# Second pass of the attention scores as two half-height products

## What is computed

```python
q, k, v = (_split_heads(query @ W) for W in (Wq, Wk, Wv))
w = jnp.einsum('bhqd,bhkd->bhqk', q, k) / DH
w = w + causal[None, None]
w = jax.nn.softmax(w, axis=-1)
mask = jnp.clip((tmpl + span_val * attn_span) / (RAMP + 1), 0.0, 1.0)
w = w * mask
w = w / (jnp.sum(w, axis=-1, keepdims=True) + 1e-08)
out = jnp.einsum('bhqk,bhkd->bhqd', w, v)
return out.transpose(0, 2, 1, 3).reshape(out.shape[0], s, H * DH) @ Wo
```

## Time and profile before

| | |
|---|---|
| median of 3 runs | 3855.66 us (3855.27 to 3858.33) |
| the profiled execution | 3857.66 us |
| its span, first to last instruction | 3855.9 us |
| PE busy (matmul) | 3504.2 us, 91% |
| PEld busy (weight loads) | 3151.9 us, 82% |
| DVE busy | 3002.8 us, 78% |
| ACT busy | 2365.9 us, 61% |
| POOL busy | 820.8 us, 21% |
| mean granted TensorE clock | 0.980 |

### The profile page before, as it was taken

How to read it: one execution, slowest core, us unless ns; L and a number is a source line. 1 busy time by engine, 2 the same in 40 slices (tenths; PEclk the granted TensorE clock), 3 DMA queues, 4 the chain that set the end, 5 groups by cost and what they waited for, 6 DMA issues and landing times. The chain is left out here.

```text
span 3855.9 us, 90130 instructions
## 1 busy us (share of the span) xinstructions
PE 3504.2 (91%) x29924; PEld 3151.9 (82%) x29924; DVE 3002.8 (78%) x4884; ACT 2365.9 (61%) x5622; POOL 820.8 (21%) x830
## 2 busy tenths in 40 slices
PE   0899996999999899989989998998999999599998
PEld 0899995888788788878878887887888888499998
DVE  7899984777777777777777777777777777599996
ACT  1454543676677667667767766776776777344544
POOL 2223221111122112112211211221121121123232
PEclk8999998999999999999999999999999999799999
DMA  6111114444534444444434444444444444211110
GB/s 211 63 55 52 54 36 129 102 102 105 130 96 118 103 116 111 108 119 99 121 97 116 114 110 114 98 119 100 116 114 102 110 109 109 92 40 51 57 49 34
DMA packets 162617, 374.13 MB, mean 97 GB/s; under 512 B 19696, under 2 KB 61552, under 8 KB 161776
## 3 DMA queue, kind: packets, MB, share of 16 engines
q1 hardware_dynamic: 162288, 370.30, 37.1%
HBM read 129.31 MB, written 39.58 MB: 44 GB/s over the span
## 5 line engine op out<-in xcount | busy, mean ns | idle before, releaser
L1233 ACT ACTIVATE at_eT_hi<-at_t_ps 128x512 f16<-128x512 f32 (+3 forms) x1536 | 745.3, 492 | 564.4 <-PE at_t_ps L1145 520.2
L1314 DVE SCALAR_TENSOR_TENSOR at_eT_lo<-at_t_ps,at_eT_hi 128x512 f16<-128x512 f32 (+3 forms) x1536 | 826.1, 551 | 163.0 <-ACT at_eT_hi L1233 132.6
L1225 ACT ACTIVATE at_e_rows<-at_s_ps,at_neg_max 128x1024 f32<-128x1024 f32 (+7 forms) x1024 | 767.0, 749 | 127.2 <-DVE at_neg_max L1308 126.3
L1145 PE MATMUL at_t_ps<-at_ident,at_e_rows 128*128 128x128 f32 x4608 | 778.8, 278 | 52.0 <-DVE at_eT_lo L1314 46.6
L1308 DVE TENSOR_REDUCE at_neg_max<-at_s_ps 128x1 f32<-128x1024 f32 (+7 forms) x1024 | 766.6, 749 | 41.8 <-PE at_s_ps L1135 30.4
L1131 PE MATMUL at_s_ps<-at_kh_st,at_q_st 128*128 128x512 f32 (+2 forms) x1536 | 581.1, 378 | 52.3 <-issue 25.4
L1159 PE MATMUL at_o_ps<-at_v_cols,at_eT_hi 128*128 128x130 f16 x4608 | 608.1, 221 | 19.0 <-ACT at_o_raw L1241 17.5
L1145 PEld LDWEIGHTS at_t_ps<-at_ident,at_e_rows 128*128 128x128 f32 x4608 | 503.6, 141 | 90.8 <-DVE at_eT_lo L1314 67.3
L1159 PE MATMUL at_o_ps<-at_v_cols,at_eT_lo 128*128 128x65 f16 x4608 | 566.8, 192 | 0.0
L1132 PE MATMUL at_s_ps<-at_kl_st,at_q_st 128*128 128x512 f32 (+2 forms) x1536 | 515.1, 343 | 0.0
L1159 PEld LDWEIGHTS at_o_ps<-at_v_cols,at_eT_hi 128*128 128x128 f16 x4608 | 434.0, 98 | 35.7 <-ACT at_o_raw L1241 21.7
(11 more groups left out here) (184 smaller groups left out, 7336.7 us busy)
## 6 DMA issues: line engine op xcount, KB each, us to landing
at_kh_st<-at_k_hi SPq DMA_DIRECT2D x256, 256.0 KB, 4.4
at_kl_st<-at_k_lo SPq DMA_DIRECT2D x256, 256.0 KB, 5.9
at_w_qk<-w_qk_split SPq DMA_DIRECT2D x65, 512.0 KB, 6.2
at_q_st<-at_q_hi SPq DMA_DIRECT2D x128, 256.0 KB, 3.9
at_q_st<-at_q_lo SPq DMA_DIRECT2D x128, 256.0 KB, 4.9
at_w_v<-w_v_split SPq DMA_DIRECT2D x66, 256.0 KB, 5.7
at_w_out<-w_out_split SPq DMA_DIRECT2D x64, 256.0 KB, 5.7
ffn_x_rows<-in_L_attn_query_dram SPq DMA_DIRECT2D x32, 256.0 KB, 2.8
```

The lines of the kernel that those rows point to most:

```text
L1145: last = nc.tensor.transpose(t_ps[i % 2][:, b * P:(b + 1) * P], e_rows[:, n % 4, (k0 + b) * P:(k0 + b + 1) * P], ident[:])
L1225: nc.scalar.activation(e_rows[:, n % 4, :w], s_ps[n % 2][:, col:col + w], ACT.Exp, bias=neg_max[:, n % 4:n % 4 + 1], accum_out=e_sum[:, pa ...
L1233: nc.scalar.activation(eT[0][:, i % EBUF, :count * P], t_ps[i % 2][:, :count * P], ACT.Copy, scale=PSCALE).then_inc(sem("eT_hi"), 1)
L1314: nc.vector.scalar_tensor_tensor(out=eT[1][:, i % EBUF, :count * P], in0=t_ps[i % 2][:, :count * P], scalar=PSCALE, in1=eT[0][:, i % EBUF, ...
```

## The change

The second pass of units with two chunks is written anew; units with one chunk keep theirs. A new set of tiles, `q_low`, gets a copy of q_hi in rows 64 to 127. In a two-chunk unit all first-pass products come first, then the mask product, then two products of 64 rows each: chunk 0 with q_hi and k_lo from rows 0 to 63 (`q_st`, `kl_st`), chunk 1 with q_hi and k_lo from rows 64 to 127 (`q_low`, `kl_st`). They write different banks of `s_ps`. The term q_lo k_lo is no longer added in these units. `place` issues two more copies for each pair, between those of q_lo and the wait for k_lo, and PE's counts for `q_placed` rise from 4 to 6 copies.

```diff
@@ -865,6 +865,7 @@
         q_st, kh_st, kl_st = ([[sb(f"{n}{i}{a}", [P, SEQ], F32R) for a in range(2)] for i in range(2)] for n in ("q_st", "kh_st", "kl_st"))
+        q_low = [[sb(f"q_low{i}{a}", [P, SEQ], F32R) for a in range(2)] for i in range(2)]
@@ -915,7 +916,7 @@
             def place(g, par):
 
-                for n, tiles in (("q", [(q_st, 0, 0), (q_st, 1, 1)]), ("k", [(kh_st, 0, 0), (kh_st, 0, 1), (kl_st, 1, 0), (kl_st, 1, 1)])):
+                for n, tiles in (("q", [(q_st, 0, 0), (q_st, 1, 1), (q_low, 0, 1)]), ("k", [(kh_st, 0, 0), (kh_st, 0, 1), (kl_st, 1, 0), (kl_st, 1, 1)])):
                     sp.wait_ge(sem(f"{n}_lo"), 2 * g + 2)
@@ -1119,20 +1120,26 @@
-                    pe.wait_ge(sem(f"q_placed{par}"), g * 32 + (64 if par == 0 else 32))
+                    pe.wait_ge(sem(f"q_placed{par}"), g * 48 + (96 if par == 0 else 48))
                     pe.wait_ge(sem(f"k_placed{par}"), g * 64 + (128 if par == 0 else 64))
 
                 pe.wait_ge(sem("exp_done"), g * NU + (n - 1 + AHEAD["exp_done"]))
                 chunks = score_chunks(j)
+                tile = slice(j * P, (j + 1) * P)
                 for ci, (col, k0, w) in enumerate(chunks):
-                    lastc = ci == len(chunks) - 1
                     out = s_ps[n % 2][:, col:col + w]
-                    qs = q_st[par][a][:, j * P:(j + 1) * P]
+                    qs = q_st[par][a][:, tile]
                     nc.tensor.matmul(out, qs, kh_st[par][a][:, k0:k0 + w], start=True, stop=False)
-                    last = nc.tensor.matmul(out, qs, kl_st[par][a][:, k0:k0 + w], start=False, stop=not lastc)
-                    if lastc:
+                    if len(chunks) == 1:
+                        nc.tensor.matmul(out, qs, kl_st[par][a][:, k0:k0 + w], start=False, stop=False)
+                    if ci == len(chunks) - 1:
                         diag = col + j * P - k0
-                        last = nc.tensor.matmul(s_ps[n % 2][:, diag:diag + P], ident_b[:], causal[:], start=False, stop=True)
+                        last = nc.tensor.matmul(s_ps[n % 2][:, diag:diag + P], ident_b[:], causal[:], start=False, stop=len(chunks) == 1)
+                if len(chunks) == 2:
+                    for ci, (col, k0, w) in enumerate(chunks):
+                        rows = slice(ci * DH, (ci + 1) * DH)
+                        last = nc.tensor.matmul(s_ps[n % 2][:, col:col + w], (q_st, q_low)[ci][par][a][rows, tile], kl_st[par][a][rows, k0:k0 + w],
+                                                start=False, stop=True)
                 last.then_inc(sem("scores_done"), 1)
```

## The result

The changed kernel takes 3939.99 us (median of 4 runs, 3939.1 to 3942.85), the kernel before beside it 3856.43: 83.6 us or 2.2% slower, ratio 1.0217, 95% interval 1.02 to 1.0235. The forecast was 3931, in a range from 3790 to 4000. The profiled execution has a span of 3937.3 us.

The account below looks back on a forecast made before the run. PE's own stream was taken as the bound. Per head 0.01 + 0.24 + 8 x 0.05 = 0.65 us, times 128 = 83, less a tenth for waits +75, plus 1 for copies: 3855.66 becomes about 3931, range 3790 to 4000.

Parts of the forecast that it names:

- column saving of 0.65 us for a head: Second passes of a head's four long tiles: fully side by side, 1.52 us becomes 0.87, saving 83 us over 128 heads.
- max(first, 0.11 + second): Pair of half products in a two-chunk unit: loads in line, so pairs take 0.23, 0.23, 0.29, 0.34 us.
- Late loads: At changes of tile no load is pulled ahead: 0.11 us shows going in, 0.06 at the transpose going out.
- the row at the mask product: Trace of the kernel before: the mask's 2-byte load begins with its product (1517.18 both), after 0.28 us of idle load path.
- the 0.32 us of the earlier trace: Kernel before, loads at 1502.77 and 1502.88: a held product starts 0.32 us from the next instead of 0.23.
- d: Time the array needs to run empty at each change of tile: taken as 0.05 us, eight changes a head.
- a tenth: PE's waits for DVE and ACT shrink when PE comes later, absorbing this share: 83 us becomes +75.
- Copies: Two more q copies per pair, some 0.6 us each, hidden with 3 us to spare; +1 us once at the start.
- (a): Rival: loads and tile changes free enough; 3821 with loads in line (chance 0.24), 3785 with loads side by side (0.13).
- (c): Rival: halves pass one after another, only changes add; 3876 with everything pulled ahead, 3986 with late loads; chance 0.06.
- (d): Rival: heavy tile changes, emptying at its upper bound of 0.16 us each; +196 us, 4050; chance 0.05.
- (b): Rival: even, changes cheap but loads late, or overlap just pays for the changes; 3848 to 3863; chance 0.09.

Follow-up runs that it names:

- the run with the mask product first: Kernel before, no half products or copies; mask product moved to the head of units following short products or transposes: 3851.0 us, ratio 0.9986.
- the run with the order alone: Changed kernel with its order and copies, but the second pass on all 128 rows: 3883.03 us, ratio 1.0072.
- mask last: Changed kernel with the mask product behind the half products instead of ahead of them: 3917.82 us, ratio 1.0162.
- pairs twice: Changed kernel with each pair of half products issued twice within one stay at half height: 4053.16 us, ratio 1.0509.

## Why the prediction was right

**The bound.** PE's stream was the bound and a change of it counted nearly in full, at an unchanged clock: right.

**Overlap.** The column saving of 0.65 us for a head was right: putting both halves on the same rows gave back 85.7 us, where 83 were computed. But the step that let the second half load follow 0.11 behind the first (a pair's time of max(first, 0.11 + second), 1.09 us a head) failed. Loads of different halves start together, and the pairs take their wider width, 0.87.

**Late loads.** No load is pulled ahead across a change of tile: right, and the row at the mask product led to it, though as an analogy it holds only behind score products (see the last section). Its size held too, 0.10 to 0.11 for a 4-byte load and 0.06 for a transpose. One reading was wrong: the 0.32 us of the earlier trace rows is not a late load. That unit follows transposes, the last of which was still passing; behind value products, where 0.32 stands as well (1509.93 to 1510.25), the load is late. The sum does not rest on it, the run with the mask product first did. The 0.05 that falls to the order of the mask product and not to the change of tile was inside the sum but in the wrong place; the run with the order alone (+23.5 us) showed it.

**Running empty.** d was put at 0.05, between 0 and 0.16. Measured 0.09 going in (mask last, the kernel in which nothing else stands there) and 0.10 going out (pairs twice). This term was mis-sized, 8 x 0.05 for a head instead of 8 x 0.095, so 46 us too small over 128 heads. Against it stood the in-line loads, 0.22 x 128 = 28 us too much, and the half load going in, put down at 0.11 where 0.10 was measured, 5 us too much. The rule of the Trainium skill, TensorEngine Tiling (Array Packing), Key Properties, that a change of mode drains TensorE, agrees with these 0.09 and 0.10 us; it gives no price.

**The sum.** Visits as measured cost 4 x 0.35 = 1.40 us a head, less 0.65 is 0.75, times 128 is 96 us; of the measured 83.6 us the copies are about 4, so 79 of the 96 arrived, and waits took a sixth of it, where a tenth was put down. Where they did can be added up from the two traces: from the first score product to the end of the transposes the units with two chunks take 92 us more, and the start of these units comes 12 us later behind the work ahead of it; the units with one chunk, which the change leaves alone, take about 18 us less, because their transposes start sooner behind the mask product (22 us less in all). The forecast's visits of 1.30 us a head, less 0.65, gave 83. That 3931 and 3940 lie so near is thus partly luck: two terms erred in opposite directions.

**Copies.** Hidden in the steady stretch, as said: right. The queue's wait for k in the changed kernel is still there:

```profile
SPq L923 <- DVE at_k_lo L1283: 190.4, 63, 3.3
```

3 us for each pair remain. At the very start they cost 2.4 us, not 1.

**Rivals.** (a), no stop at the changes, fell with the 0.16 and 0.43 us of one unit. (c), no overlap, fell with the halves on one set of rows: its 3986 would have been 4026 with the visits at their measured price. (d), d at its upper bound, fell with the pairs issued twice. (b) would have needed visits at about 0.16 us on average (0.65 a head over four visits), and they cost 0.35.

## What to carry to other kernels

Half-height products side by side do save their columns in full, but a visit to half height has a fixed price, here 0.28 us where a mask product stood ahead anyway and up to 0.38 between two 4-byte products. The columns that overlap in one visit must be worth more than that (by 0.23 us for 512 columns, an estimate is some 620 to 850 columns; no run here had a form that paid), so gather the half-height work into few long visits; one pair per unit is too little. The pairs issued twice show that more work in a visit adds no second price. And ask of every move of a short product what load stood hidden behind its neighbours, and whether that neighbour is shorter than the load of 0.11 us at all: moving the mask product to the middle cost 23.5 us by itself.

## What was not expected of the hardware

Two weight loads for different halves start at the same time (both 1513.90), while two loads for whole height stand 0.11 us apart. The change to half height costs 0.09 us and the change back 0.10, and that only for the tile. The 2-byte load of the mask product is held back behind a 4-byte score product as well, but this costs no pause, not even right behind a half product, where the mask product passed in 0.06. It is not the change of weight size alone that holds it: behind a 4-byte transpose the same load is pulled ahead by a median of 0.11 us (119 units of the kernel with the mask product first), and behind every score product of the kernel before it begins within 0.01 us of its product. Why the two differ is open.
